# A fused attention and expert kernel: the convolution stage's operations in another order on three engines, and the row of maxima from a one-column stationary side

## The chip, the cores and the metric

The kernel runs on one core of one Trainium2 chip. A core has a matrix engine (TensorE, PE in the profile), three engines for elementwise work (VectorE or DVE, ScalarE or ACT, GpSimd or POOL), and a queue engine (SyncE or SP) that issues most of the DMAs. Each engine works through its own instructions strictly in the order in which they are written, and waits on semaphores for the others. The metric is the device time of one execution in microseconds (us), lower is better.

## The reference, cut to what matters

The input `x` has 8 images of 128 channels and 32x32 positions. A block with attention is added to it, then a block with routed experts. The change touches the attention block and where it meets the routing of the image before:

```python
inp = _ln_c(x) + 2.0 * sinu                     # per position, over channels
q = conv2d(inp, wq)                             # 1x1
k = conv2d(inp, wk, 1, 1); v = conv2d(inp, wv, 1, 1)   # 3x3, 128 -> 256 channels
q = q * cos + rotate_every_two(q) * sin         # the same for k
dots = einsum('bhid,bhjd->bhij', q, k) * SCALE  # 8 heads, 1024 x 1024 each
attn = softmax(dots, axis=-1)                   # subtracts each row's maximum
attn = einsum('bhij,hg->bgij', attn, mix)
out = einsum('bhij,bhjd->bhid', attn, v)        # then wo, bias and a sigmoid gate
x = x + a * sigmoid(g)                          # then tokens, router, two experts of 8
```

## The kernel before, in words

All matmuls are made precise by splitting every fp32 operand into a high part (`...h`, rounded to the engine's fast fp32 format) and a rest (`...l`), with three products instead of four. A copy on ScalarE makes the high part, a subtraction on VectorE the rest.

The eight images are eight batches of a loop (batch 0 stands alone in front of it, without the work on a batch before it). Each batch has two stages:

* **The convolution stage.** `conv_q` makes q in four pieces, `conv(b, cg, i)` the 3x3 convolutions in a Winograd form along x: `cg` is 0 and 1 for k's two halves of channels, 2 and 3 for v; `i` is one of four transformed components, each in its own bank of `ST`. A component is 9 matmuls for k and 18 for v. ScalarE copies component 0 out (`middle_copy`), VectorE joins the others (`middle_sums`, then `even_odd` for the even and the odd positions). For q and k, VectorE and GpSimd apply the rotary tables (`rotate` or `turn`, eight groups g: 0 to 3 are q, 4 to 7 are k), ScalarE and VectorE split the result (`rot_hi`, `rot_lo`) and SP spills it to DRAM (`stk`), from which `stacks` loads the operands of a head (`qst`, `kst`). Head 0 needs groups 0 to 5. For v, `v_hi` and `v_lo` split it in place. Woven into this stage is what is left of the batch before: `out_transpose`, `out_hi`/`out_lo`, `out_project`, `gate_tanh`/`gate`, `route_in`, `row_transposed`, `logits`, and the clearing of the accumulator `acc`.
* **The attention stage**, 32 units (8 heads by 4 blocks of 256 query rows), two heads to a call of `pair`. For each unit `max_scores` makes scores with the queries as the output's rows, `take_max` takes each row's maximum into `mcol`, `max_row` turns the column of maxima into a row by a matmul with a negative identity, ScalarE copies that row into `qst` (`row_copy`), `scores` makes the scores again, transposed and with the maximum subtracted, `exps` and `exp_lo` take exponentials and split them, `values` multiplies by v in 48 matmuls and `normalise` adds to the output through GpSimd.

The first two units' maxima and the first unit's scores and exponentials are made inside the convolution stage, between the components of v. `values` of unit 0 starts when all of v is split (`wait(pe, s_vlo, split)`). The order on each engine is written out by hand in the function `batch` of that engine; nothing reorders it later. Each engine's `batch` calls the helpers named above; the waits in them (`wait_ge`) count semaphore steps.

Of the kernel before, what the change touches and what calls it, by code (L numbers as in the profile page):

```python
# [43 lines left out]
def build(nc, x, wq, wk, wv, mix, wo, bo, wr, br, ln_g, ln_b, w1, b1, w2, b2,  # L44
# [19 lines left out]
    with ctx:  # L64
# [96 lines left out]
        mcol = a_sb("mcol", [P, 2, 2, P], f32r)  # L161
# [216 lines left out]
        def _(sp):  # L378
# [49 lines left out]
            def fill(i):  # L428
                if i == 0:
                    wait(sp, s_const, 11)  # L430
# [107 lines left out]
        def _(pool):  # L538
# [11 lines left out]
            nc.gpsimd.memset(f(mcol[:, :, :, :]), 0.0).then_inc(s_const, 1)  # L550
# [5 lines left out]
            pool.wait_ge(s_const, 11)  # L556
# [149 lines left out]
        def _(pe):  # L706
# [227 lines left out]
            def batch(b):  # L934
                prev = None if isinstance(b, int) else b - 1
                n = b * UNITS
                for g in range(4):
                    conv_q(b, g)
                if prev is not None:
                    out_transpose(prev, 0)  # L940
                conv(b, 0, 0)
                conv(b, 0, 1)
# [21 lines left out]
                max_row(n, 0)  # L964
                if prev is not None:
# [4 lines left out]
                conv(b, 3, 2)  # L970
                scores(n, 0, 0, b)
                conv(b, 3, 3)
                max_scores(n + 1, 1, 1)
                scores(n, 0, 1, b)
# [13 lines left out]
            pe.wait_ge(s_const, 8)  # L988
# [109 lines left out]
        def _(act):  # L1098
# [3 lines left out]
            act.wait_ge(s_const, 8)  # L1102
# [106 lines left out]
            def batch(b):  # L1209
                prev = None if isinstance(b, int) else b - 1  # L1210
                rot_hi(b, 0)
                if prev is not None:
                    out_hi(prev, 0)
                rot_hi(b, 1)
                rot_hi(b, 2)
                middle_copy(b, 0)
                rot_hi(b, 3)
                if prev is not None:
                    gate_tanh(prev, 0)
                    out_hi(prev, 1)  # L1220
                middle_copy(b, 1)
# [8 lines left out]
                rot_hi(b, 7)  # L1230
# [618 lines left out]
```

## Time and profile before

| | |
|---|---|
| time, median of 3 runs | 3048.92 us (3046.03 to 3050.79) |
| the profiled execution's own time | 3044.3 us |
| its span | 3042.6 us |
| TensorE busy | 2841.2 us (93%) |
| VectorE busy | 2269.0 us (75%) |
| ScalarE, GpSimd busy | 1469.0 us, 1395.8 us |
| mean granted TensorE clock | 0.969 of full speed |
| convolution stage of batch 1 | 358.2 to 421.5 us |
| the same stage of batch 2 | 683.7 to 747.0 us |

The span is the time from the first to the last instruction of the profiled execution. Batches 1 to 7 repeat each other every 326 us; after 2640 us follow the experts, which the change does not touch. A stage is taken here from the first matmul of `conv_q` to the first of `values`. Matmul rows overlap, so the time that a matmul takes of the engine is the distance between starts, not its duration. The granted clock is a share of full speed: 1.00 is 2.4 GHz, 0.50 is 1.2 GHz.

### The profile page before, as it was taken

The page shows a single profiled execution, that of the slowest core. Times are in us where ns is not written, and L with a number is a line of the kernel's source. Part 1 is how long each engine was busy: PE and PEld are TensorE (multiplying, and loading weights), DVE is VectorE, ACT ScalarE, POOL GpSimd, SP SyncE. Part 2 cuts the span into 40 slices and gives each one's busy share as a digit, 9 for nine tenths or more (in the row PEclk, how much of TensorE's full clock was granted, in tenths as well). Part 3 has the DMA queues.
Part 4 walks back from the last instruction along what each step waited for, and adds up shares of the span by engine and source line. Part 5 has one row for each costly group of instructions (what it writes and reads, how often), then busy time and mean ns, then how long its engine had stood idle before and what let it go on. Part 6 is the DMA issues. An engine that isn't in the chain of part 4 may idle for free.

```text
span 3042.6 us, 54782 instructions
## 1 busy us (share of the span) xinstructions
PE 2841.2 (93%) x20238; PEld 2665.9 (88%) x20238; DVE 2269.0 (75%) x3470; ACT 1469.0 (48%) x1884; POOL 1395.8 (46%) x1056
## 2 busy tenths in 40 slices
PE   6999989998999899999999899989998999958996
PEld 5899889997999899988998899979997999847776
DVE  6677778777877787777877787778777887655663
ACT  2455435543555355534554355535553455435771
POOL 4244524543454434552464245443455246336883
PEclk9999999999999999999999999999999999969998
DMA  2555020102010210102010211020011111137665
GB/s 110 189 195 200 29 73 22 37 18 91 22 38 26 77 36 24 41 31 72 22 45 11 89 32 30 25 91 22 25 39 56 47 32 59 43 115 250 231 223 210
DMA packets 88838, 230.51 MB, mean 76 GB/s; under 512 B 17160, under 2 KB 17746, under 8 KB 88566
## 3 DMA queue, kind: packets, MB, share of 16 engines
q1 hardware_dynamic: 79478, 209.96, 20.5%
q0 software_dynamic: 9088, 16.94, 1.7%
q8 instruction: 169, 2.77, 0.4%
q14 instruction: 103, 0.84, 0.1%
HBM read 90.76 MB, written 96.89 MB: 62 GB/s over the span
## 4 chain that ended last, share of the span: by engine, by line
PE 73%; issue 7%; DVE 7%; POOL 4%; DMA 4%; ACT 3%; SPq 1%; DVEq 0%; POOLq 0%; ACTq 0%
PE PV L708 46%; PE ST L708 14%; PE MX L708 12%; DMA wt<-wall 2%; DVE rt L1417 1%; POOL acc L587 1%; DVE ul L1370 1%; ACT h L1100 1%; DMA qst<-stk 1%; DMA stk<-rt 1%; ACT xr L1100 1%; DVE mcol L1448 1%; POOL rt L580 1%; POOL E L595 1%; POOL E L593 1%
## 5 line engine op out<-in xcount | busy, mean ns | idle before, releaser
L587 POOL TENSOR_TENSOR acc<-acc,tmp 128x256 f32<-128x256 f32 x512 | 802.8, 1568 | 1282.6 <-DVE tmp L1463 1280.3
L708 PE MATMUL PV<-vh,El 128*128 128x258 f32 x4096 | 1189.7, 290 | 27.5 <-DVE vl L1443 22.1
L708 PE MATMUL PV<-vh,Eh 128*128 128x258 f32 x4096 | 1162.1, 284 | 0.0
L708 PE MATMUL PV<-vl,Eh 128*128 128x256 f32 x4096 | 1152.2, 281 | 0.0
L1100 ACT ACTIVATE Eh<-ST 128x1024 fp32r<-128x1024 f32 x512 | 526.2, 1028 | 765.1 <-PE ST L708 765.1
L1448 DVE TENSOR_REDUCE mcol<-MX 128x1 fp32r<-128x1024 f32 x512 | 625.8, 1222 | 313.4 <-PE MX L708 310.6
L708 PEld LDWEIGHTS PV<-vh,El 128*128 128x128 f32 x4096 | 777.6, 190 | 59.4 <-DVE vl L1443 20.5
L708 PEld LDWEIGHTS PV<-vl,Eh 128*128 128x128 f32 x4096 | 783.4, 191 | 25.5 <-issue 3.8
L708 PEld LDWEIGHTS PV<-vh,Eh 128*128 128x128 f32 x4096 | 777.4, 190 | 0.0
L1453 DVE TENSOR_TENSOR El<-E,Eh 128x1024 fp32r<-128x1024 f32 x512 | 635.2, 1241 | 0.0
L1100 ACT ACTIVATE E<-ST 128x1024 f32<-128x1024 f32 x512 | 522.2, 1020 | 0.0
L708 PE MATMUL MX<-kst,qst 96*128 96x512 f32 x1024 | 331.2, 405 | 28.6 <-DMA qst<-stk 28.6
L708 PE MATMUL ST<-qst,kst 97*128 97x256 f32 x2048 | 343.2, 290 | 9.7 <-ACT qst L1100 6.7
L708 PEld LDWEIGHTS ST<-qst,kst 97*128 97x128 f32 x2048 | 281.7, 191 | 17.7 <-issue 9.5
L1463 DVE SCALAR_TENSOR_TENSOR tmp<-PV,rl,mix_sb 128x256 f32<-128x256 f32 x512 | 247.7, 484 | 18.8 <-DVE rl L1459 1.0
L674 POOL DMA_INDIRECT yrows<-xr,idx x156 | 189.6, 1216 | 76.5 <-issue 41.0
L1100 ACT ACTIVATE qst<-MX 1x256 fp32r<-1x256 f32 x256 | 96.8, 378 | 263.8 <-PE MX L708 263.3
L708 PEld LDWEIGHTS MX<-kst,qst 96*128 96x128 f32 x1024 | 160.7, 193 | 30.4 <-DMA qst<-stk 30.2
L1747 DVE TENSOR_TENSOR hl<-h,hh 128x1024 fp32r<-128x1024 f32 x78 | 95.7, 1227 | 102.6 <-ACT hh L1100 82.3
L1459 DVE RECIPROCAL rl<-PV 128x1 f32<-128x1 f32 x512 | 85.5, 167 | 102.3 <-PE PV L708 100.6
L593 POOL TENSOR_TENSOR E<-E,sin_sb 128x512 f32<-128x512 f32 x64 | 85.5, 1336 | 142.3 <-DVE E L1413 99.3
L611 POOL DMA_INDIRECT rows<-xr,slot x128 | 126.8, 991 | 27.0 <-issue 15.5
(245 smaller groups left out, 3476.8 us busy)
## 6 DMA issues: line engine op xcount, KB each, us to landing
rows<-xr SPq DMA_DIRECT2D x68, 520.0 KB, 6.2
stk<-rt SPq DMA_DIRECT2D x64, 512.0 KB, 2.7
kst<-stk SPq DMA_DIRECT2D x192, 128.0 KB
qst<-stk SPq DMA_DIRECT2D x192, 128.0 KB
wt<-wall SPq DMA_DIRECT2D x39, 514.0 KB
wt<-wall SPq DMA_DIRECT2D x39, 512.5 KB
xrow<-rows SPq DMA_DIRECT2D x39, 260.0 KB
wall<-yrows SPq DMA_DIRECT2D x32, 256.0 KB, 4.6
```

The source lines that it names most:

```text
L580: nc.gpsimd.tensor_tensor(u[3][:, :, 0:last], even[:, :, 0:last], even[:, :, 1:HALFW], ALU.subtract)
L587: nc.gpsimd.tensor_tensor(acc[:, ic, :], acc[:, ic, :], tmp[:, p, :], ALU.add).then_inc(s_acc, 1)
L593: nc.gpsimd.tensor_tensor(s, s, table(sin_sb, g), ALU.mult).then_inc(s_rot, 1)
L611: nc.gpsimd.indirect_dma_start(out=rows_d[:, :], out_offset=bass.IndirectOffsetOnAxis(ap=slot[:, i:i + 1], axis=0), in_=xr[c][:, g, :], in ...
L674: nc.gpsimd.indirect_dma_start(out=yrows_d[:, :], out_offset=bass.IndirectOffsetOnAxis(ap=idx[j % XR][:, i:i + 1], axis=0), in_=yrow[j % Y ...
L708: return nc.tensor.matmul(o, w, m, start=start, stop=stop)
L1100: return nc.scalar.activation(o, i, func, **kw)
L1448: nc.vector.tensor_reduce(mcol[:, k % 2, p, MROW:MROW + 1], MX[:, :], AX, ALU.max).then_inc(s_red, 1)
L1453: tt(El[at].rearrange("p a b -> p (a b)"), E32[:, p, :], f(Eh[at]).rearrange("p a b -> p (a b)"), ALU.subtract).then_inc(s_lo, 1)
L1459: nc.vector.reciprocal(rl[:, p:p + 1], PV[p][:, INNER:INNER + 1]).then_inc(s_rl, 1)
L1463: stt(tmp[:, p, :].rearrange("p (g d) -> p g d", d=DH), PV[p][:, 0:INNER].rearrange("p (g d) -> p g d", d=DH), rl[:, p:p + 1], m, ALU.mult ...
L1747: tt(low, exact, f(high), ALU.subtract).then_inc(t_hl, 1)
```

## The change

Three things are changed, and nothing in what is computed.

First, `mcol` holds only the maxima, two by two columns, where before it held a 128-column block for each with the maxima in column 96 and zeros elsewhere. `max_row` so loads one column as its stationary side and writes one row of `MX` (row 0) where it wrote 128 rows. The clearing of the block on GpSimd is gone, and the counts of `s_const` fall by one.

Second, `even_odd` is no longer called within `turn`; the clearing of `acc` is a function `clear`.

Third, the calls in the three `batch` functions stand in another order. Before and after (cut to the calls; those of the batch before have `prev`):

```diff
--- TensorE, batch(b)
-                for g in range(4):
-                    conv_q(b, g)
+                conv_q(b, 0)
+                conv_q(b, 1)
                     out_transpose(prev, 0)
+                conv_q(b, 2)
+                conv_q(b, 3)
                 conv(b, 0, 0)
+                    out_transpose(prev, 1)
                 conv(b, 0, 1)
                     out_project(prev, 0)
-                    out_transpose(prev, 1)
                 conv(b, 0, 2)
                 conv(b, 0, 3)
                 conv(b, 1, 0)
                 conv(b, 1, 1)
+                conv(b, 1, 2)
                     out_project(prev, 1)
-                conv(b, 1, 2)
                 conv(b, 1, 3)
                 conv(b, 2, 0)
                     route_in(prev)
                 conv(b, 2, 1)
+                conv(b, 2, 2)
+                conv(b, 2, 3)
                 max_scores(n, 0, 0, b * 384 + 96)
-                conv(b, 2, 2)
+                conv(b, 3, 0)
                 max_scores(n, 0, 1)
-                conv(b, 2, 3)
+                conv(b, 3, 1)
                 max_row(n, 0)
-                conv(b, 3, 0)
-                max_scores(n + 1, 1, 0)
-                conv(b, 3, 1)
                 conv(b, 3, 2)
                 scores(n, 0, 0, b)
+                max_scores(n + 1, 1, 0)
                 conv(b, 3, 3)
-                max_scores(n + 1, 1, 1)
                 scores(n, 0, 1, b)
+                max_scores(n + 1, 1, 1)
--- TensorE, max_row(n, k)
-                    last = mm(MX[:, p * P:(p + 1) * P], mcol[:, k % 2, p, :], negid[:, :], True, True)
+                    last = mm(MX[0:1, p * P:(p + 1) * P], mcol[:, k % 2, p:p + 1], negid[:, :], True, True)
--- ScalarE, row_copy(n, k)
-                copy(qst[st][MROW:MROW + 1, q * QT:(q + 1) * QT], MX[MROW:MROW + 1, 0:QT]).then_inc(s_mrow, 1)
+                copy(qst[st][MROW:MROW + 1, q * QT:(q + 1) * QT], MX[0:1, 0:QT]).then_inc(s_mrow, 1)
--- ScalarE, batch(b)
-                rot_hi(b, 0)
                     out_hi(prev, 0)
+                middle_copy(b, 0)
+                rot_hi(b, 0)
                 rot_hi(b, 1)
-                rot_hi(b, 2)
-                middle_copy(b, 0)
-                rot_hi(b, 3)
                     gate_tanh(prev, 0)
+                rot_hi(b, 2)
                     out_hi(prev, 1)
+                rot_hi(b, 3)
                 middle_copy(b, 1)
...
-                rot_hi(b, 7)
-                row_copy(b * UNITS, 0)
                 v_hi(b, 0)
                 v_hi(b, 1)
+                rot_hi(b, 7)
                 middle_copy(b, 3)
+                row_copy(b * UNITS, 0)
+                v_hi(b, 2)
+                act.wait_ge(s_rlo, b * 8 + 7)
                 exps(b * UNITS, 0, 0)
-                v_hi(b, 2)
                 v_hi(b, 3)
+                act.wait_ge(s_rlo, b * 8 + 8)
                 exps(b * UNITS, 0, 1)
--- VectorE, clear(n) and batch(b)
+            def clear(n):
+                wait(dve, s_tr, n * 4 + 4)
+                nc.vector.memset(acc[:, :, :], 0.0)
                 rotate(b, 0)
-                for g in range(1, 4):
-                    rotate(b, g)
-                    rot_lo(b, g - 1)
-                    if g == 1 and prev is not None:
-                        out_lo(prev, 0)
-                rot_lo(b, 3)
+                    out_lo(prev, 0)
+                rotate(b, 1)
+                    clear(prev)
+                rot_lo(b, 0)
+                rotate(b, 2)
+                rot_lo(b, 1)
+                rotate(b, 3)
                 middle_sums(b, 0)
+                even_odd(b, 0, 0)
+                rot_lo(b, 2)
                     gate(prev, 0)
+                turn(b, 4)
+                rot_lo(b, 3)
                     out_lo(prev, 1)
-                turn(b, 4)
+                even_odd(b, 0, 1)
                 turn(b, 5)
                 middle_sums(b, 1)
-                rot_lo(b, 4)
                     gate(prev, 1)
+                rot_lo(b, 4)
+                even_odd(b, 1, 0)
+                even_odd(b, 1, 1)
                 rot_lo(b, 5)
                 turn(b, 6)
                 turn(b, 7)
-                rot_lo(b, 6)
+                middle_sums(b, 2)
+                even_odd(b, 2, 0)
                     logits(prev)
+                rot_lo(b, 6)
+                v_lo(b, 0)
+                even_odd(b, 2, 1)
                 take_max(n, 0, 0)
-                middle_sums(b, 2)
+                v_lo(b, 1)
                 rot_lo(b, 7)
-                even_odd(b, 2, 0)
                 take_max(n, 0, 1)
-                even_odd(b, 2, 1)
-                    wait(dve, s_tr, prev * 4 + 4)
-                    nc.vector.memset(acc[:, :, :], 0.0)
-                v_lo(b, 0)
-                take_max(n + 1, 1, 0)
-                v_lo(b, 1)
                 middle_sums(b, 3)
                 even_odd(b, 3, 0)
+                take_max(n + 1, 1, 0)
+                v_lo(b, 2)
                 even_odd(b, 3, 1)
                 exp_lo(n, 0, 0)
-                v_lo(b, 2)
+                v_lo(b, 3)
                 take_max(n + 1, 1, 1)
-                v_lo(b, 3)
                 exp_lo(n, 0, 1)
```

How the instructions stand now is shown at three places of a batch of the loop. On VectorE at the head of the stage, from `rotate(b, 0)` on (`El<-PV` is `out_lo`, `rt<-E,rt` is `rot_lo`, `MEMSET acc` the clearing; ISA and REGISTER_ALU are the waits' own instructions), before:

```order
L1387 TENSOR_TENSOR E<-ST,cos_sb 128x512
L1388 STREAM_SHUFFLE E<-ST 128x512
L41 REGISTER_ALU
L1387 TENSOR_TENSOR E<-ST,cos_sb 128x512
L1388 STREAM_SHUFFLE E<-ST 128x512
L41 ISA
L1417 TENSOR_TENSOR rt<-E,rt 128x512
L41 ISA
L1424 TENSOR_TENSOR El<-PV,Eh 128x512
L41 REGISTER_ALU
L1424 TENSOR_TENSOR El<-PV,Eh 128x512
L41 REGISTER_ALU
```

After, from the shuffle of `rotate(b, 0)` on:

```order
L1393 STREAM_SHUFFLE E<-ST 128x512
L41 ISA
L1428 TENSOR_TENSOR El<-PV,Eh 128x512
L41 REGISTER_ALU
L1428 TENSOR_TENSOR El<-PV,Eh 128x512
L41 REGISTER_ALU
L1392 TENSOR_TENSOR E<-ST,cos_sb 128x512
L1393 STREAM_SHUFFLE E<-ST 128x512
L41 REGISTER_ALU
L1482 MEMSET acc 128x2048
L41 ISA
L1421 TENSOR_TENSOR rt<-E,rt 128x512
```

The two `out_lo` now stand before `rotate(b, 1)`, and the clearing, which stood behind both `even_odd(b, 2, ...)`, stands before the first `rot_lo`.

On VectorE at the end of the stage, from `middle_sums(b, 3)` on, before (`vl<-vt,vh` is `v_lo`, `mcol<-MX` is `take_max`, `El<-E,Eh` is `exp_lo`; `vt<-vt,ST` closes as `even_odd(b, 3, 1)`):

```order
L1394 TENSOR_TENSOR vt<-vt,ST 128x512
L1395 TENSOR_TENSOR vt<-vt,ST 128x512
L1399 REGISTER_ALU
L1402 TENSOR_TENSOR vt<-ST,vt 128x512
L1399 REGISTER_ALU
L1404 TENSOR_TENSOR vt<-vt,ST 128x512
L1453 TENSOR_TENSOR El<-E,Eh 128x1024
L1443 TENSOR_TENSOR vl<-vt,vh 128x512
L41 REGISTER_ALU
L1448 TENSOR_REDUCE mcol<-MX 128x1
L1443 TENSOR_TENSOR vl<-vt,vh 128x512
L1453 TENSOR_TENSOR El<-E,Eh 128x1024
```

After, from `even_odd(b, 3, 0)` on:

```order
L1407 TENSOR_TENSOR vt<-ST,vt 128x512
L41 ISA
L1452 TENSOR_REDUCE mcol<-MX 128x1
L1447 TENSOR_TENSOR vl<-vt,vh 128x512
L1404 REGISTER_ALU
L1409 TENSOR_TENSOR vt<-vt,ST 128x512
L1457 TENSOR_TENSOR El<-E,Eh 128x1024
L1447 TENSOR_TENSOR vl<-vt,vh 128x512
L41 REGISTER_ALU
L1452 TENSOR_REDUCE mcol<-MX 128x1
L1457 TENSOR_TENSOR El<-E,Eh 128x1024
```

Between `even_odd(b, 3, 1)` and the last `v_lo` stood an `exp_lo`, a `v_lo` and a `take_max`; now only the `exp_lo` stands there.

On TensorE at the end of the stage, from the last matmul of `conv(b, 3, 3)` to the first of `values`, before (`MX<-kst,qst` is `max_scores`, `ST<-qst,kst` is `scores`):

```order
L708 MATMUL ST<-wch,uh 128x256
L41 ISA
L708 MATMUL MX<-kst,qst 128x512 x2
L883 REGISTER_ALU
L708 MATMUL ST<-qst,kst 128x256 x4
L708 MATMUL PV<-vh,El 128x258
```

After:

```order
L707 MATMUL ST<-wch,uh 128x256
L882 REGISTER_ALU
L707 MATMUL ST<-qst,kst 128x256 x4
L41 ISA
L707 MATMUL MX<-kst,qst 128x512 x2
L707 MATMUL PV<-vh,El 128x258
```

`scores(n, 0, 1)` and `max_scores(n + 1, 1, 1)` have changed places.

## Rows read from the trace of the kernel before

**Rows 1.** Page, part 1: engine, busy us (share of the span), instructions.

```profile
PE 2841.2 (93%) x20238; PEld 2665.9 (88%) x20238; DVE 2269.0 (75%) x3470; ACT 1469.0 (48%) x1884; POOL 1395.8 (46%) x1056
```

**Rows 2.** Windows of batch 1: busy us of PE, PEld, DVE, ACT, POOL; PEclk, DMA, GB/s.

```profile
397.00:404.90 7.90, 5.58 (x22) 5.30 (x23) 4.65 (x7) 1.90 (x3) 2.45 (x2) 0.57 0.39 133
...
421.50:427.50 6.00, 6.00 (x35) 5.91 (x36) 2.44 (x3) 2.32 (x3) 0.00 (x0) 0.72 0.01 3
440.00:620.00 180.00, 179.04 (x1405) 174.53 (x1404) 146.31 (x228) 99.25 (x122) 90.28 (x62) 1.00 0.12 34
```

**Rows 3.** Waits of TensorE, whole run: total us, times, longest.

```profile
PE MX L708 <- DMA qst<-stk: 28.6, 8, 7.2
PE PV L708 <- DVE vl L1443: 22.1, 8, 2.9
```

**Rows 4.** Timeline of PE, batch 1: start, us, instruction, count [idle before <- releaser].

```profile
358.22 0.39 PE L708 MATMUL ST<-xl,wqh 128*128 128x512 f32 x1
...
399.32 1.22 PE L708 MATMUL MX<-kst,qst 96*128 96x512 f32 x2 [3.37 <-DMA qst<-stk]
400.33 0.41 PE L708 MATMUL ST<-wcl,uh 128*128 128x256 f32 x1
...
416.26 0.28 PE L708 MATMUL ST<-wch,uh 128*128 128x256 f32 x1
416.38 0.28 PE L708 MATMUL ST<-wcl,uh 128*128 128x256 f32 x1
...
418.03 0.74 PE L708 MATMUL ST<-qst,kst 97*128 97x256 f32 x4 [0.31 <-DVE vt L1404]
421.50 0.39 PE L708 MATMUL PV<-vh,El 128*128 128x258 f32 x1 [2.73 <-DVE vl L1443]
```

**Rows 5.** Timeline of DVE, same batch: the low half of group 5.

```profile
390.81 0.68 DVE L1417 TENSOR_TENSOR rt<-E,rt 128x512 fp32r<-128x512 f32 x1
```

**Rows 6.** Timeline of DVE: end of the stage.

```profile
417.29 0.69 DVE L1404 TENSOR_TENSOR vt<-vt,ST 128x512 f32<-128x512 f32 x1 [2.17 <-PE ST L708]
...
419.64 1.22 DVE L1448 TENSOR_REDUCE mcol<-MX 128x1 fp32r<-128x1024 f32 x1
420.77 0.68 DVE L1443 TENSOR_TENSOR vl<-vt,vh 128x512 fp32r<-128x512 f32 x1
```

**Rows 7.** Timeline of DVE: waits at the head, and the clearing.

```profile
360.62 0.68 DVE L1387 TENSOR_TENSOR E<-ST,cos_sb 128x512 f32<-128x512 f32 x1
...
365.47 1.03 DVE L1417 TENSOR_TENSOR rt<-E,rt 128x512 fp32r<-128x512 f32 x1 [2.27 <-ACT rt L1100]
...
372.82 1.01 DVE L1417 TENSOR_TENSOR rt<-E,rt 128x512 fp32r<-128x512 f32 x1 [1.83 <-ACT rt L1100]
...
408.34 1.76 DVE L1642 MEMSET acc<- 128x2048 f32 x1 [0.38 <-issue]
```

**Rows 8.** Timeline of DVE and POOL: two that meet.

```profile
387.22 1.82 DVE L1417 TENSOR_TENSOR rt<-E,rt 128x512 fp32r<-128x512 f32 x1
...
387.20 1.29 POOL L595 TENSOR_TENSOR E<-E 128x512 f32<-128x512 f32 x1
```

**Rows 9.** Timeline of PE round the row of maxima, full clock.

```profile
345.21 0.28 PE L708 MATMUL PV<-vh,Eh 128*128 128x258 f32 x1
345.34 0.33 PE L708 MATMUL MX<-negid,mcol 128*128 128x128 f32 x2
345.51 0.33 PE L708 MATMUL PV<-vh,El 128*128 128x258 f32 x1
345.68 0.28 PE L708 MATMUL PV<-vl,Eh 128*128 128x256 f32 x1
```

**Rows 10.** Windows of 75 us, one for each batch's stage.

```profile
358.20:433.20 75.00, 65.31 (x393) 57.90 (x392) 55.16 (x88) 22.49 (x34) 27.17 (x20) 0.93 0.27 92
...
1336.30:1411.30 75.00, 65.72 (x381) 58.02 (x381) 52.05 (x82) 22.10 (x33) 25.31 (x19) 0.91 0.27 92
```

**Rows 11.** Groups of weight loads: busy us, mean ns of one.

```profile
L708 PEld LDWEIGHTS MX<-negid,mcol 128*128 128x128 f32 x512 | 80.7, 192 | 0.0
```

More of the change, by code:

```diff
@@ L160, in build @@
         xg = a_sb("xg", [P, TOK], f32)
[L161 removed]
+        mcol = a_sb("mcol", [P, 2, 2], f32r)
         negid = a_sb("negid", [P, P], f32r)
@@ L429, in fill @@
                 if i == 0:
-                    wait(sp, s_const, 11)
+                    wait(sp, s_const, 10)
                 sp.dma_start(rows_d[i * FILL:(i + 1) * FILL, :].rearrange("(p r) c -> p (r c)", r=KC),
@@ L936, in batch @@
                 n = b * UNITS
-                for g in range(4):
-                    conv_q(b, g)
+                conv_q(b, 0)
+                conv_q(b, 1)
                 if prev is not None:
                     out_transpose(prev, 0)
+                conv_q(b, 2)
+                conv_q(b, 3)
                 conv(b, 0, 0)
+                if prev is not None:
+                    out_transpose(prev, 1)
                 conv(b, 0, 1)
@@ L960, in batch @@
                 max_scores(n, 0, 0, b * 384 + 96)
-                conv(b, 2, 2)
+                conv(b, 3, 0)
                 max_scores(n, 0, 1)
-                conv(b, 2, 3)
+                conv(b, 3, 1)
                 max_row(n, 0)
+                conv(b, 3, 2)
+                scores(n, 0, 0, b)
+                max_scores(n + 1, 1, 0)
+                conv(b, 3, 3)
+                scores(n, 0, 1, b)
+                max_scores(n + 1, 1, 1)
                 if prev is not None:
                     pe.wait_ge(s_lg, b + 0)
-                conv(b, 3, 0)
-                max_scores(n + 1, 1, 0)
-                conv(b, 3, 1)
-                conv(b, 3, 2)
-                scores(n, 0, 0, b)
-                conv(b, 3, 3)
-                max_scores(n + 1, 1, 1)
-                scores(n, 0, 1, b)
                 def heads_next(hp):
@@ L1210, in batch @@
                 prev = None if isinstance(b, int) else b - 1
-                rot_hi(b, 0)
                 if prev is not None:
                     out_hi(prev, 0)
+                middle_copy(b, 0)
+                rot_hi(b, 0)
                 rot_hi(b, 1)
-                rot_hi(b, 2)
-                middle_copy(b, 0)
-                rot_hi(b, 3)
                 if prev is not None:
                     gate_tanh(prev, 0)
+                rot_hi(b, 2)
+                if prev is not None:
                     out_hi(prev, 1)
+                rot_hi(b, 3)
                 middle_copy(b, 1)
@@ L1408, in turn @@
                 cg, odd = g // 2 - 2, g % 2
-                even_odd(b, cg, odd)
                 dve.wait_ge(s_rlo, b * 8 + g - 1)
@@ L1611, in batch @@
                 rotate(b, 0)
-                for g in range(1, 4):
-                    rotate(b, g)
-                    rot_lo(b, g - 1)
-                    if g == 1 and prev is not None:
-                        out_lo(prev, 0)
-                rot_lo(b, 3)
+                if prev is not None:
+                    out_lo(prev, 0)
+                rotate(b, 1)
+                if prev is not None:
+                    clear(prev)
[3 more added lines that the diff above has]
+                rotate(b, 3)
                 middle_sums(b, 0)
+                even_odd(b, 0, 0)
+                rot_lo(b, 2)
                 if prev is not None:
                     gate(prev, 0)
+                turn(b, 4)
+                rot_lo(b, 3)
+                if prev is not None:
                     out_lo(prev, 1)
-                turn(b, 4)
+                even_odd(b, 0, 1)
                 turn(b, 5)
                 middle_sums(b, 1)
-                rot_lo(b, 4)
                 if prev is not None:
                     gate(prev, 1)
+                rot_lo(b, 4)
+                even_odd(b, 1, 0)
+                even_odd(b, 1, 1)
                 rot_lo(b, 5)
```

10 lines of the change are left out of this document (4 added, 6 removed).

## The prediction

> **What bounds the kernel now.** First the page's part 1: TensorE is busy for 93% of the span, VectorE for 75% [rows 1]. Such shares are means over unlike stages, so next the windows by stage. In the attention loop TensorE is busy for 179.0 of 180 us at a granted clock of 1.00, VectorE for 146 [rows 2]: there only fewer or shorter matmuls count, and what VectorE or ScalarE do costs nothing. The convolution stage is different. The waits of TensorE over the whole run name two of its places, one each per batch: `max_scores` of unit 0 for the loads of head 0 (28.6 us in 8 waits) and the first `values` for the last low half of v (22.1 us in 8) [rows 3]. The timeline shows both in batch 1, 3.37 us ahead of 399.32 and 2.73 us ahead of 421.50 [rows 4]. Behind each the clock falls: 0.57 in the window that begins with the first wait, 0.72 behind the second [rows 2]. The stage goes from 358.22 to 421.50, 63.3 us [rows 4], eight times.
>
> **The head of the stage: reordered, worth nothing by itself.** It ends when `qst` and `kst` of head 0 have landed. That is 7.83 us (399.32 - 391.49) after VectorE ends the low half of group 5, at 390.81 + 0.68 [rows 4, 5]. So the question is when VectorE gets there. It starts at 360.62 and takes 30.9 us to that end, with waits of 2.27 and 1.83 us for ScalarE among them, and a third of the second's size [rows 7]; some 6 us in all. The new order puts more in front of that point: the clearing (1.7 us of the engine by its row of 1.76 [rows 7]) and both `even_odd(b, 1, ...)` (0.61 us each, the distance between starts of two such operations of 512 columns), 2.9 us. In return other work fills the old waits: `out_lo(prev, 0)` stands where `rotate(b, 0)` is being finished by GpSimd and ScalarE. One wait is new: `clear` needs all of `out_transpose(prev, 1)`, which on TensorE stands behind the transposes of the first half, two `conv_q` and `conv(b, 0, 0)` (0.85 + 1.4 + 2.05 us, from the starts of such matmuls in the timeline). I make that wait 1.7 us; behind it stand `rot_lo(b, 0)` and with it `rotate(b, 2)`, for which `conv(b, 0, 2)` waits, another 0.7 us on TensorE. With 2.9 added, about 2 of new waits and about 5 of old ones filled, VectorE ends group 5 when it did, to within 1.5 us. I take zero: the landing stays where it was.
>
> A rule of the Trainium skill, "SBUF — State Buffer", section "Who interferes with whom", speaks to this: the port pair that VectorE and GpSimd share is an exclusive lock, taken by a VectorE operation with two inputs in SBUF, and the later of the two stands still. The trace agrees: a `rot_lo` that takes 0.68 us elsewhere [rows 5] took 1.82 when GpSimd had started 1.29 us of work 0.02 us before it [rows 8]. The clearing now meets GpSimd's rotary work, and I take it to hold the lock like the others. By the rule a memset, which has no input, takes none; then the landing is about 1 us earlier than I take it, and the sum below would be 8 us less.
>
> **Between the landing and the first `values`: here is the gain.** Before, 22.2 us (399.32 to 421.50). A component of v is 18 matmuls at 0.12 us from start to start (416.26 to 416.38 [rows 4]), 2.14 us; four `max_scores` and two `scores` are 0.47 each, `max_row` 0.2. So 6 x 2.14 + 2.8 + 0.2 = 15.8 us of matmuls, waits of 0.31 + 2.73 = 3.0, some 2.7 lost to the low clock, 0.7 for latencies. After, `conv(b, 2, 2)` and `conv(b, 2, 3)` stand ahead of the landing, where TensorE waited: 4 x 2.14 + 3.0 = 11.6 us of matmuls remain. Their 4.3 us eat the old wait of 3.4 and what the head gives TensorE; I leave 1.1 us of wait there. Waits behind the landing, in the new order: `max_scores(n, 0, 1)` for `take_max(n, 0, 0)`, now behind `even_odd(b, 2, 1)`, 0.7; `scores(n, 0, 1)` directly behind `conv(b, 3, 3)` for `even_odd(b, 3, 1)`, 1.0; `values` for the last `v_lo`, 0.8. The last comes from VectorE's tail: from 417.29 to 421.45 before [rows 6], of which `v_lo` (0.61) and `take_max` (1.13, 419.64 to 420.77) no longer stand ahead of the last `v_lo`. Sum after: 11.6 + 2.5 + 0.7 = 14.8 us. Against 22.2 - 2.7 = 19.5 that is 4.7 us a batch without the clock. What was passed is late next: `take_max(n + 1, 1, 1)` comes after the start of `values`, and the `max_row` in it waits 0.4 us. Seven batches at 4.3 are 30 us. Batch 0, which had the longest wait of the eight (7.2 us [rows 3]), I put at 6. Together **36 us**.
>
> **The clock.** A window of 75 us over each stage has a mean granted clock of 0.93 (0.91 in one) [rows 10]: 75 x 0.07 = 5.2 us of full-clock time, 43 us over eight stages. Some of it falls into the waits themselves; what matmuls lose is about 34 us. It follows the two long waits. With 1.1 for 3.4 us at the first and three short ones for 2.7 at the second I expect most of it back, but not all, since the sparse matmuls of `route_in` and the short waits remain. Between 0 and 34 I take **20 us**.
>
> **The row of maxima.** 256 units. Before, from the start of its two matmuls to that of the second matmul behind them is 0.34 us, of which one matmul of 258 columns accounts for 0.12: the pair costs 0.22 [rows 9]. No row of this trace has a stationary side of one column. If loading it costs as before, nothing is gained. If it costs nothing, the pair is as long as its 256 moving columns, 0.12, and 0.10 us a unit or 26 us is gained. The matmul behind the pair still loads 128 columns, which 128 moving columns hardly cover; so I take the middle, 0.05 us, **13 us**.
> The Trainium skill, "TensorE: Matmul & The Clock Gate", section "LDWEIGHTS (loading the stationary operand)", has the load's time grow with its columns, 128 of them at 1.2 per ns, an estimate of 0.11 us. No row here shows one of another width. By it two of three loads vanish, and the saving would be 0.06 us a unit, 15 us.
>
> `row_copy` reads as many elements as before. The memset that goes on GpSimd lies in the setup, beside the loading of the weights: nothing.
>
> **Sum.** 36 + 20 + 13 = 69 us. The profiled execution took 3044.3 us, 4.6 below the median of 3048.92 and inside the spread of the runs. 3044.3 - 69 = **2975 us**.
>
> **The rivals.**
> A. The clock stays. The short waits that replace the long ones, with `route_in` between them, leave the clock as it was, and a narrow load costs what a wide one did. For it: the row at 0.91 against 0.93 [rows 10] shows that a stage can lose more with much the same waits. Against it: each low stretch of rows 2 begins at a wait of about 3 us. Time: 3044.3 - 36 = 3008.
> B. More than I take. The landing comes 1 us earlier, all of the clock returns, a unit saves 0.1: 44 + 34 + 26 = 104 us, 2940.
> C. The head becomes the bound. `clear` holds `rot_lo(b, 0)`, and what is behind it, for longer than the old waits give back, so that head 0 lands later by some 4 us. For it: that wait is new and in front of everything; against it: the 6 us that VectorE idled there. Each us later costs 8: 36 + 13 - 32 = 17, so 3027 with the clock unchanged. It would take 8 us a batch to undo all.
> D. Slower: the narrow load. A weight load is 192 ns long in its rows [rows 11] and runs beside the matmul ahead of it. If a load of one column, or the wide one behind it, can't be made ahead, each unit pays up to 2 x 0.19 us: 256 x 0.38 = 97 us. With 56 us of the other gains: 3044.3 - 56 + 97 = 3085. It decides from 0.22 us a unit on. For it speaks only that no row shows such a load.
> That the reordering does nothing at all would need the wait for `stk` to move with it; it doesn't hang on TensorE's order.
>
> **How the numbers follow.** My forecast 0.72, with its own range of 2955 to 2995 (head 1.5 us either way, 12 us; clock and row each by a third); A 0.13; B 0.07; C 0.05; D 0.03. The range from 2947 to 3012 takes in most of B and all of A. About 0.2% (6 us) is what a measurement of this kernel can tell from no change. Faster by more: 0.95; within it 0.02, from the edge between C and D; slower 0.03, D.
>
> **What would show it.** In the changed profile: the stage of batch 1 about 55 us long instead of 63.3; the wait of `MX` for `qst<-stk` about 1 us a batch, so 8 to 12 in all instead of 28.6, and that of `PV` for `vl` about 6 instead of 22; a wait of VectorE ahead of the clearing near 1.7 us; 14 to 16 us from the first `max_scores` to the first `values`; a granted clock of 0.96 or more in the 75 us; a unit of the attention loop shorter by about 0.05 us. I am wrong if the low half of group 5 ends more than 32.5 us after `rotate(b, 0)` starts, if the clock falls as often as before, or if a unit has become longer.

## The result, and the profile after

| | before | after |
|---|---|---|
| time, median of 4 runs each | 3047.48 us (3045.1 to 3050.79) | 2947.55 us (2941.37 to 2948.00) |
| profiled execution, its span | 3044.3, 3042.6 us | 2941.37, 2939.6 us |
| its mean granted clock | 0.969 | 0.983 |

The ratio is 0.9667, its interval 0.9652 to 0.9681: 100 us less, where my sum had 69 and the forecast was 2975 us. The time lies at the very edge of my range (2947) and outside the likeliest case's own (2955 to 2995). Counted from the 3044.3 us from which I had subtracted, the ratio gives 3044.3 x 0.9667 = 2943 us, and the profiled execution took 2941.37: both lie below the range. The direction and the places are as forecast, the size is that of rival B.

Part 1 of the page of after, beside [rows 1]:

```profile
PE 2785.8 (95%) x20238; PEld 2605.9 (89%) x20238; DVE 2268.5 (77%) x3470; ACT 1468.3 (50%) x1884; POOL 1405.3 (48%) x1055
```

TensorE's busy time is 55 us less with the same 20238 matmuls; the other half of the 103 us of span is idle time that is gone. 55 us less of busy time for the same work is already a hint at the clock and at the cheaper row. The profiled execution is the fastest of the four; the others had a mean clock of 0.981 and took 6 us more, so they may well hold a low stretch or two that this trace doesn't show.

Windows of batch 1 of after (busy us of PE, PEld, DVE, ACT, POOL; then clock, DMA share, GB/s). They answer to [rows 2], the last three to [rows 10]:

```profile
389.30:397.20 7.90, 7.84 (x63) 7.63 (x64) 5.61 (x8) 2.12 (x4) 0.00 (x0) 1.00 0.35 130
402.70:408.70 6.00, 5.83 (x46) 5.57 (x47) 4.79 (x6) 3.29 (x5) 0.53 (x1) 1.00 0.33 74
420.00:600.00 180.00, 178.95 (x1417) 173.81 (x1415) 147.64 (x229) 99.15 (x122) 91.03 (x63) 1.00 0.12 34
347.80:422.80 75.00, 70.15 (x465) 62.85 (x465) 64.04 (x108) 28.16 (x41) 29.60 (x22) 1.00 0.28 92
661.80:736.80 75.00, 70.59 (x464) 62.83 (x465) 62.68 (x105) 28.20 (x41) 30.27 (x22) 1.00 0.28 92
1289.40:1364.40 75.00, 70.55 (x463) 62.66 (x464) 62.75 (x105) 28.07 (x41) 30.48 (x22) 1.00 0.28 92
```

The two windows that stood at 0.57 and 0.72 stand at 1.00, and so do the 75 us of a stage that stood at 0.93 and 0.91. In the first, TensorE starts 63 matmuls in 7.9 us, where it started 22 before. The loop's 180 us are as full as they were; its matmuls are 1417 where they were 1405 in the same time, which is the cheaper row.

Waits of TensorE in after, beside [rows 3] (total us, times, longest):

```profile
PE MX L707 <- DMA qst<-stk: 10.5, 8, 3.2
PE ST L707 <- DVE E L1393: 10.2, 13, 1.4
...
PE ST L707 <- DVE vt L1409: 6.2, 8, 0.8
...
PE PV L707 <- DVE vl L1447: 4.8, 8, 0.7
...
PE MX L835 <- DVE xg L1441: 1.4, 1, 1.4
...
PE MX L707 <- DVE El L1428: 0.3, 1, 0.3
```

28.6 has become 10.5 and 22.1 has become 4.8; `scores(n, 0, 1)` now waits for `even_odd(b, 3, 1)`, eight times 0.8. The last two rows, together 1.7, are waits of the stage's head for work of the batch before; in the profile of before they were 7.7 and 15.2:

```profile
PE MX L708 <- DVE El L1424: 15.2, 14, 1.4
...
PE MX L836 <- DVE xg L1437: 7.7, 8, 1.4
```

I had not looked at these, since a longer wait stood behind them. They come back below.

TensorE's timeline, batch 1 of after: start, us, instruction, count [idle before <- releaser]. It answers to [rows 4]:

```profile
347.85 0.39 PE L707 MATMUL ST<-xl,wqh 128*128 128x512 f32 x1
...
351.24 1.09 PE L815 MATMUL PV<-ident,acc 128*128 128x128 f32 x8 [1.84 <-POOL acc L586]
...
372.00 0.49 PE L707 MATMUL MX<-El,woh 128*128 128x512 f32 x1 [0.35 <-DVE El L1428]
...
389.36 0.73 PE L707 MATMUL MX<-kst,qst 96*128 96x512 f32 x2 [1.09 <-DMA qst<-stk]
...
391.94 0.28 PE L707 MATMUL ST<-wch,uh 128*128 128x256 f32 x1
392.06 0.63 PE L707 MATMUL MX<-kst,qst 96*128 96x512 f32 x2
...
400.95 0.74 PE L707 MATMUL ST<-qst,kst 97*128 97x256 f32 x4 [0.78 <-DVE vt L1409]
401.53 0.63 PE L707 MATMUL MX<-kst,qst 96*128 96x512 f32 x2
402.74 0.36 PE L707 MATMUL PV<-vh,El 128*128 128x258 f32 x1 [0.58 <-DVE vl L1447]
```

The stage is 402.74 - 347.85 = 54.9 us long; 55 was forecast, for 63.3. The wait ahead of the first `max_scores` is 1.09, forecast 1.1. From there to `values` it is 13.38 us, forecast 14.8. `max_scores(n, 0, 1)`, at 392.06, follows the convolution with no wait at all.

VectorE in the same batch, beside [rows 5 to 8], and two rows of GpSimd:

```profile
350.25 0.68 DVE L1392 TENSOR_TENSOR E<-ST,cos_sb 128x512 f32<-128x512 f32 x1
...
357.13 1.76 DVE L1482 MEMSET acc<- 128x2048 f32 x1 [2.01 <-PE PV L815]
...
365.72 1.51 DVE L1436 TENSOR_SCALAR tmp<-tmp 128x512 f32<-128x512 f32 x1
...
380.68 0.69 DVE L1421 TENSOR_TENSOR rt<-E,rt 128x512 fp32r<-128x512 f32 x1
...
401.95 0.69 DVE L1447 TENSOR_TENSOR vl<-vt,vh 128x512 fp32r<-128x512 f32 x1
```

```profile
356.55 1.30 POOL L594 TENSOR_TENSOR E<-E 128x512 f32<-128x512 f32 x1
...
365.33 1.62 POOL L594 TENSOR_TENSOR E<-E 128x512 f32<-128x512 f32 x1
```

The clearing waits 2.01 us for the transposes (forecast 1.7), and the low half of group 5 ends 381.37 - 350.25 = 31.1 us after `rotate(b, 0)` starts, where it took 30.9: in this batch the head costs VectorE nothing, as forecast. The load lands 7.99 us later (7.83 before). Batch 1 is not like the others, though. In batches 2 to 7 the same way is 30.0 us long, where it was 30.9 in every batch of before, and the clearing waits less:

```profile
670.26 1.76 DVE L1482 MEMSET acc<- 128x2048 f32 x1 [1.29 <-PE PV L815]
```

To compare the variants I use three distances, from the starts in TensorE's timeline, as means over batches 1 to 7: from the stage's first matmul to the first `max_scores` ("to the landing"), from there to the first `values`, and from there to the third `max_row` (for e4 over six batches, since a record is missing in batch 4).

| us | to the landing | to `values` | stage | to third `max_row` | batch to batch |
|---|---|---|---|---|---|
| before | 42.05 | 21.52 | 63.57 | 18.91 | 326.20 |
| after | 41.30 | 13.39 | 54.68 | 17.13 | 313.88 |
| e1_row_only | 42.19 | 21.68 | 63.87 | 18.53 | 324.41 |
| e2_order_only | 41.34 | 13.45 | 54.78 | 17.49 | 316.24 |
| e3_filled | 44.99 | 19.73 | 64.71 | 16.94 | 325.54 |
| e4_early_max | 41.30 | 20.12 | 61.42 | 17.13 | 321.05 |
| e5_filled_ahead | 42.44 | 19.80 | 62.24 | 16.94 | 322.91 |
| e6_old_tail | 41.28 | 15.12 | 56.40 | 18.20 | 316.79 |
| e7_old_head | 43.56 | 14.20 | 57.76 | 17.29 | 317.33 |
| e8_clear_later | 41.83 | 13.38 | 55.21 | 17.31 | 314.88 |

### The profile page after: what moved, and what is told of

Same layout as the page of the kernel before. It is cut to its first block, busy times and chain, and to the rows that moved or that the text cites. A ratio compares the mean times of both kernels' runs of the same rounds, so it can differ in the third digit from the quotient of the medians.

```text
span 2939.6 us, 54790 instructions
## 1 busy us (share of the span) xinstructions
PE 2785.8 (95%) x20238; PEld 2605.9 (89%) x20238; DVE 2268.5 (77%) x3470; ACT 1468.3 (50%) x1884; POOL 1405.3 (48%) x1055
## 3 DMA queue, kind: packets, MB, share of 16 engines
q0 software_dynamic: 9088, 16.94, 1.8%
## 4 chain that ended last, share of the span: by engine, by line
PE 74%; DVE 8%; issue 5%; POOL 5%; DMA 4%; ACT 2%; SPq 1%; DVEq 0%; POOLq 0%; ACTq 0%
PE PV L707 48%; PE ST L707 14%; PE MX L707 11%; DMA wt<-wall 2%; DVE rt L1421 1%; POOL acc L586 1%; POOL E L594 1%; DVE ul L1375 1%; DMA qst<-stk 1%; DMA stk<-rt 1%; ACT xr L1102 1%; DVE El L1457 1%; POOL rt L579 1%; POOL E L592 1%; DMA wall<-yrows 0%
## 5 line engine op out<-in xcount | busy, mean ns | idle before, releaser
L707 PE MATMUL ST<-qst,kst 97*128 97x256 f32 x2048 | 337.0, 286 | 13.6 <-ACT qst L1102 7.4
L707 PE MATMUL MX<-kst,qst 96*128 96x512 f32 x1024 | 324.4, 398 | 10.5 <-DMA qst<-stk 10.5
```

Of the source, the lines that this page charges most:

```text
L707: return nc.tensor.matmul(o, w, m, start=start, stop=stop)
```

## The experiments

The median of before beside the first four was 3044.22 us, beside the other four 3044.38. My theory is that of the prediction, with larger sizes; the rivals are named in each expectation.

**The two parts, each alone.** `e1_row_only` is before with the one-column side alone; `e2_order_only` is after with the 128-column side put back:

```diff
--- e1_row_only, in before (mcol, row_copy and take_max to match)
-                    last = mm(MX[:, p * P:(p + 1) * P], mcol[:, k % 2, p, :], negid[:, :], True, True)
+                    last = mm(MX[0:1, p * P:(p + 1) * P], mcol[:, k % 2, p:p + 1], negid[:, :], True, True)
--- e2_order_only, in after: the same line the other way
```

> The kernel before with the one-column stationary side alone, order untouched. Theory (the narrow load is cheap): a unit of the attention loop, 7.90 us before and 7.83 in the changed kernel, becomes 7.83 here too; 256 units by 0.07 us is 18 us, so a ratio to before near 0.994, and the stage of batch 1 stays 63 us. Rival (the shorter unit comes from the order, the narrow side is worth nothing): ratio 1.000, unit 7.90.

> The changed order with the old 128-column stationary side. Theory: it gives what the whole change gives less 18 us: 2966 us, ratio 0.973; the stage of batch 1 54.9 us, no low clock in batches 1 to 7, a unit 7.90. If parts help each other (the short load keeps the clock up), low stretches come back here and the ratio is above 0.98.

Measured: e1 3027.81 us, ratio 0.9946 (0.9933 to 0.9959), 16 us less than before; e2 2965.48 us, 0.9743 (0.9728 to 0.9758), 79 us less. They add up: 16 + 79 = 95 of 100 us, within what the intervals (some 5 us each) can tell. So the row is worth 16 us in before and, between e2 and after, 18 (medians) to 23 (ratios). The place, in e1's timeline of TensorE, beside [rows 9]:

```profile
502.16 0.28 PE L707 MATMUL PV<-vh,Eh 128*128 128x258 f32 x1
502.28 0.28 PE L707 MATMUL MX<-negid,mcol 128*1 128x128 f32 x2
502.39 0.34 PE L707 MATMUL PV<-vh,El 128*128 128x258 f32 x1
502.56 0.28 PE L707 MATMUL PV<-vl,Eh 128*128 128x256 f32 x1
```

From the matmul ahead of the pair to the second behind it are 502.56 - 502.16 = 0.40 us, where [rows 9] have 0.47. That is 0.07 us a unit, 256 x 0.07 = 18 us. I had measured from the pair's own start and so left out 0.01 us ahead of it; the rest is that the middle of my bounds was a little low. The weight load, in the groups of after, beside [rows 11] (busy us, mean ns | idle):

```profile
L707 PEld LDWEIGHTS MX<-negid,mcol 128*1 128x1 f32 x512 | 41.4, 82 | 11.1 <-DVE mcol L1452 2.5
```

It lasts 82 ns where it lasted 192. By the Trainium skill, "TensorE: Matmul & The Clock Gate", section "LDWEIGHTS (loading the stationary operand)", 127 columns less at 1.2 per ns would be an estimated 106 ns less; the two rows differ by 110, so the trace agrees. Rival D is refuted: the pair has become shorter and not longer.

In one point e2 is not as expected: two of its seven windows of 75 us over a stage stand at 0.98 and not at 1.00. In batch 3 the low stretch is at the head of the stage, in batch 5 behind `values`, though the waits of these two stages (1.00 and 1.28, 0.78, 0.58 us) are about those of the other five.

**Is it the waits or the clock?** `e3_filled` and `e5_filled_ahead` are before with matmuls added whose result nobody reads, so that TensorE does not stand still at its two long waits:

```diff
+            def filler(count):
+                for i in range(count):
+                    mm(PV[1][:, :], wqh[:, 0:P], xh[:, 0:NB], True, True)
...
+                filler(12 if prev is not None else 28)      # e5: here
                 if prev is not None:
                     pe.wait_ge(s_xr, b + 0)
+                filler(13 if prev is not None else 29)      # e3: here instead
                 max_scores(n, 0, 0, b * 384 + 96)
...
                 scores(n, 0, 1, b)
+                filler(10)                                  # both
```

> The kernel before in its old order, with matmuls whose results nobody reads put into the two long waits of TensorE (13 of 512 columns ahead of the first max_scores, 29 in batch 0, and 10 ahead of the first values; 0.23 us each at full clock, so shorter than the waits of 3.4, 7.2 and 2.7 us). Nothing else is moved. Theory (the waits pull the clock down, and the low clock costs matmul time behind them): most of the 43 us by which the clock falls short over eight stages comes back, 25 to 34 us of it as time: 3015 to 3022 us, ratio 0.990 to 0.992, stage of batch 1 about 60.5 us. Rival (the clock falls for another reason, or what it costs is hidden by VectorE): ratio 0.999 to 1.001.

> The kernel before in its old order, with unread matmuls again, now ahead of TensorE's wait for ScalarE's copy of MX as well (in e3 they stood behind it, started 2.4 us late and ended after the loads of head 0 had landed): 12 of 512 columns ahead of that wait (28 in batch 0), 10 ahead of the first values. Theory (the waits pull the clock down and the low clock costs matmul time): the granted clock falls in fewer stages, the stage of batch 1 is 60.5 to 61 us, and of the 43 us lost in the clock 25 to 34 come back: 3012 to 3020 us, ratio 0.989 to 0.992. Rival (the low clock costs less, since TensorE waits for VectorE behind it anyway): the 15 us of e3 again, ratio 0.995.

Measured: e3 3028.8 us, 0.9949 (0.9933 to 0.9964), a miss by 7 us at least. The row that shows why, TensorE's timeline of e3:

```profile
395.79 2.50 PE L708 MATMUL PV<-xh,wqh 128*128 128x512 f32 x5 [2.38 <-ACT xr L1106]
```

My fillers stood behind TensorE's wait for ScalarE's `xr` copy, the `s_xr` of the diff. The profile of before puts the whole idle time down to the DMA, which came last; another semaphore was waited for in the same gap. So TensorE stood still for 2.38 us in spite of the fillers, and these then ran past the landing, which the table has at 44.99 instead of 42.05. So the total prices neither the waits nor the clock. The table does show the stretch behind the landing: 19.73 us to `values` instead of 21.52, and 16.94 instead of 18.91 from there.

e5 has them ahead of that wait: 3018.16 us, 0.9906 (0.9891 to 0.9921), as the theory had it (the stage of batch 1, 61.3 us, is a little longer than expected): 26 us less than before by the medians and 29 by the ratio, with more matmuls to do and the same work behind the same loads. Its timeline and its windows of 75 us over the stages of batches 1 and 3:

```profile
392.52 2.91 PE L708 MATMUL PV<-xh,wqh 128*128 128x512 f32 x12
396.44 0.74 PE L708 MATMUL MX<-kst,qst 96*128 96x512 f32 x2 [1.02 <-DMA qst<-stk]
```

```profile
354.90:429.90 75.00, 69.90 (x439) 60.97 (x439) 58.19 (x96) 24.45 (x36) 27.42 (x21) 1.00 0.27 92
...
999.70:1074.70 75.00, 69.82 (x425) 61.26 (x426) 55.54 (x88) 24.29 (x36) 26.55 (x20) 0.98 0.27 92
```

With the wait cut to 1.02 us the clock stays at 1.00 in five of the seven stages. That is shown, then: TensorE's standing still in the two long waits brings most of the low clock, and the low clock alone is worth 26 to 29 us here. This is a lower bound, for two reasons. Two stages (batches 3 and 6) still have a short stretch of it ahead of the landing, although no wait of over 1.8 us is in them. And the fillers push the first `max_scores` back by 0.4 us (42.44 for 42.05), some 3 us in the whole. The table gives the same size behind the landing: (21.52 - 19.80) + (18.91 - 16.94) = 3.7 us a batch, some 29 us in eight.

And since e5 and e2 both have the wide row and (nearly) no low clock, their distance is the worth of the order by itself: 3018.2 - 2965.5 = 53 us by the medians, 50 by the ratios; the 3 us of the fillers are in it, so it is rather 47 to 50.

**Two components of v ahead of the landing.** `e4_early_max` is after with the first `max_scores` back ahead of them:

```diff
-                conv(b, 2, 2)
-                conv(b, 2, 3)
                 if prev is not None:
                     pe.wait_ge(s_xr, b + 0)
                 max_scores(n, 0, 0, b * 384 + 96)
+                conv(b, 2, 2)
+                conv(b, 2, 3)
```

> The changed kernel with the first max_scores back ahead of conv(b, 2, 2), all else as changed. Theory (two components of v ahead of the landing are the main gain): TensorE waits 1.1 + 4.3 = 5.4 us there, low clock returns at that wait; 8 x 4.3 = 34 us and 15 to 20 for the clock: about 2998 us, ratio 0.983. Rival (the gain is in the tail and in the clock of the second wait): 2950 us, ratio 0.968.

Measured: 2998.41 us, 0.9853 (0.9834 to 0.9872), as expected: 51 to 57 us of the 100 hang on this one move. Timeline and window of its batch 1:

```profile
393.81 1.22 PE L707 MATMUL MX<-kst,qst 96*128 96x512 f32 x2 [5.51 <-DMA qst<-stk]
```

```profile
352.10:427.10 75.00, 65.72 (x410) 58.55 (x409) 56.58 (x93) 24.59 (x36) 26.63 (x20) 0.95 0.27 92
```

The landing has not moved (41.30 in both); what was work is a wait again, and behind the wait the clock falls.

**VectorE's tail.** `e6_old_tail` is after with the end of VectorE's stage as it was:

```diff
                 take_max(n + 1, 1, 0)
-                v_lo(b, 2)
                 even_odd(b, 3, 1)
                 exp_lo(n, 0, 0)
-                v_lo(b, 3)
+                v_lo(b, 2)
                 take_max(n + 1, 1, 1)
+                v_lo(b, 3)
                 exp_lo(n, 0, 1)
```

> The changed kernel with VectorE's old tail: v_lo(b, 2) and take_max(n + 1, 1, 1) back between even_odd(b, 3, 1) and v_lo(b, 3). Theory: the first values waits 2.3 instead of 0.58 us, 1.7 us in each of 8 batches is 14 us, and a low stretch returns behind that wait for 8 to 12 more: 2968 to 2974 us, ratio 0.975 to 0.977. If the tail's order is worth its own 1.7 us only, 2961 us, ratio 0.972. Rival (all of the gain is in the two components ahead of the landing): 2948 us, ratio 0.967.

Measured: 2971.91 us, 0.9755 (0.9742 to 0.9769), 24 us above after, or 27 by the ratios, as the theory had it.

```profile
408.25 0.56 PE L707 MATMUL PV<-vh,El 128*128 128x258 f32 x1 [2.31 <-DVE vl L1447]
```

```profile
407.70:413.70 6.00, 5.45 (x33) 5.30 (x34) 2.81 (x3) 2.15 (x3) 0.00 (x0) 0.72 0.13 29
```

The wait of `values` is 2.31 us instead of 0.58, which is 8 x 1.7 = 14 us, and the window behind it stands at 0.72, as the one of before did. The clock's part is again nearly as large as the wait's. It is not bound to each wait: in batch 5, with the same wait of 2.31 us, the clock stayed at 1.00.

**The head.** `e7_old_head` is after with the old head on all three engines, the clearing behind `rot_lo(b, 5)`; `e8_clear_later` is after with the clearing behind `rot_lo(b, 1)`:

```diff
--- e7_old_head, TensorE (ScalarE and VectorE likewise)
+                for g in range(4):
+                    conv_q(b, g)
                     out_transpose(prev, 0)
                 conv(b, 0, 0)
                 conv(b, 0, 1)
                     out_project(prev, 0)
+                    out_transpose(prev, 1)
...
+                    out_project(prev, 1)
                 conv(b, 1, 2)
--- e8_clear_later, VectorE
                 rotate(b, 1)
-                    clear(prev)
                 rot_lo(b, 0)
                 rotate(b, 2)
                 rot_lo(b, 1)
+                    clear(prev)
                 rotate(b, 3)
```

> The changed kernel with the old order of the head on TensorE, ScalarE and VectorE, up to the low half of group 5, turns with even_odd inside again, and the clearing right behind that low half. Theory of the prediction (the head's reordering moves nothing but the clearing): the loads land when they did, 41 to 42 us into the stage, but the clearing and both even_odd of k's second half now stand behind the landing's release and make groups 6 and 7 and take_max late, 2 to 2.5 us a batch: 2964 to 2970 us, ratio 0.974. Rival (the new head is what makes the rest early): the landing is 3 us or more later and the time above 2985 us, ratio above 0.98.

> The changed kernel with the clearing of acc behind rot_lo(b, 1) instead of ahead of rot_lo(b, 0), where VectorE waits 2.01 us for the transposes. Theory (GpSimd and ScalarE, not VectorE, set when groups 2 to 5 are done; the wait only moves to rot_lo(b, 0) and to conv(b, 0, 3)): same time within 3 us, 2945 to 2951. Rival (that wait is on the path to the landing): the landing comes up to 2 us earlier, TensorE's 1.1 us there go, 9 to 15 us less: 2933 to 2939 us, ratio 0.963.

Measured: e7 2972.53 us, 0.9754 (0.9739 to 0.9769), 25 us above after; e8 2952.31 us, 0.9691 (0.9677 to 0.9704), 5 us above it (7 by the ratios), at the edge of what can be told. So a later clearing does not bring the landing forward (41.83 against 41.30), and the wait ahead of the clearing costs nothing. e7 is the more telling one. It is a miss for both of its sides: 2.5 us above the theory's times, with the first `max_scores` at 43.56 and not at 41 to 42, and 12 us below the rival's. Waits with a bracket, and the first `max_scores`, in its batch 1:

```profile
352.52 1.10 PE L815 MATMUL PV<-ident,acc 128*128 128x128 f32 x8 [0.47 <-POOL acc L586]
358.62 0.50 PE L707 MATMUL MX<-El,woh 128*128 128x512 f32 x1 [0.90 <-DVE El L1424]
371.72 0.49 PE L707 MATMUL MX<-El,woh 128*128 128x512 f32 x1 [0.93 <-DVE El L1424]
381.83 1.09 PE L835 MATMUL MX<-ident,xg 128*128 128x128 f32 x8 [0.90 <-DVE xg L1437]
392.46 0.63 PE L707 MATMUL MX<-kst,qst 96*128 96x512 f32 x2
```

The first `max_scores` (392.46) has no wait for its loads any more: with the old head and two components more in front of it, TensorE itself gets there last. Now the small waits of the head count in full, 3.2 us in this batch, which in before were hidden in the wait for the landing. The new head has 1.84 + 0.35 = 2.2. Of the 2.9 us between the two arrivals (43.35 and 41.51 less the 1.09 of wait) these are 1.0; 7.4 x 0.22 = 1.6 are clock, which falls in this batch with hardly a wait:

```profile
379.00:385.00 6.00, 5.11 (x45) 4.90 (x44) 5.55 (x7) 0.63 (x1) 0.38 (x1) 0.98 0.46 175
385.00:392.40 7.40, 7.40 (x52) 7.40 (x52) 6.42 (x13) 2.62 (x4) 5.48 (x4) 0.78 0.38 106
```

Batches 2 to 6 are another case, and the more frequent one. Rows of batch 2, whose stage begins at 665.50:

```profile
675.84 0.50 PE L707 MATMUL MX<-El,woh 128*128 128x512 f32 x1 [1.40 <-DVE El L1424]
...
708.71 0.72 PE L707 MATMUL MX<-kst,qst 96*128 96x512 f32 x2 [0.40 <-ACT xr L1099]
712.39 0.72 PE L707 MATMUL MX<-kst,qst 96*128 96x512 f32 x2 [0.82 <-DVE mcol L1448]
```

The small waits of its head sum up to 3.9 us where batch 2 of after has 1.4, and that is 2.5 of the 2.7 us by which TensorE gets to the first `max_scores` later (42.8 us into the stage against 40.1). There it waits for ScalarE's `xr` copy and not for the loads, and the second `max_scores` waits for VectorE's `take_max`; both come late because of what now stands behind `rot_lo(b, 5)` on VectorE, as the theory had it for `take_max`: ahead of `xr` ScalarE copies out a component of v, and for that it waits 9.1 us for VectorE's `turn`, until 40.9 us into the stage (35.7 in after). With the wait for the landing (1.17) gone, that makes 1.9 us more to the first `max_scores` and 1.1 us more from there to `values`.

## Why the prediction was right in kind and wrong in size

By measured parts, in us (the parts were run on two occasions, so sums agree only to a few us):

| term | predicted | measured | from |
|---|---|---|---|
| order, without the clock | 36 | 50 to 53 (3 of them the fillers') | e5 against e2 |
| clock | 20 | 26 to 29 at least | before against e5 |
| row of maxima | 13 | 16 to 23 | e1; e2 against after |
| sum | 69 | 92 to 105 | the whole: 100 |

**The step that failed first: "Sum after: 11.6 + 2.5 + 0.7 = 14.8 us".** The matmuls were right. The waits behind the landing were to be 0.7 + 1.0 + 0.8; they are 0 + 0.78 + 0.58. And 13.38 - 11.6 - 1.36 leaves 0.4 for the latencies, not 0.7. Each price was rounded up a little, and the 1.4 us between 14.8 and 13.4 count eight times. The 19.5 that I had for the old stretch at full clock is 19.80 in e5, another 0.3. Together 1.65 us a batch, 13 us.

**The head: "I take zero: the landing stays where it was".** For batch 1, which I had read, it nearly holds: from the first `conv_q` 41.10 before, 41.51 after. For batches 2 to 7 it doesn't: they had it at 42.0 to 42.4 before, and have it at 41.0 to 41.6 after. The low half of group 5 in batch 2, VectorE's timeline of before and of after:

```profile
717.15 0.68 DVE L1417 TENSOR_TENSOR rt<-E,rt 128x512 fp32r<-128x512 f32 x1
```

```profile
694.51 0.68 DVE L1421 TENSOR_TENSOR rt<-E,rt 128x512 fp32r<-128x512 f32 x1
```

That is 33.42 us behind the stage's first matmul (683.73) before and 32.48 behind it (662.03) after, 0.9 us less. In batch 1 it was 32.59 and 32.83. VectorE was no quicker in batch 1 of before: from `rotate(b, 0)` to group 5 it took 30.9 us there as everywhere. But `rotate(b, 0)` starts 2.40 us into that stage and 3.2 to 3.5 us into the others, and in the new order these others get to group 5 in 30.0 us, with a shorter wait ahead of the clearing (1.29 for 2.01) and one slow `TENSOR_SCALAR` where batch 1 has two (below). So I had judged seven batches by the one that is unlike the rest. In e7, with the old head, group 5 ends 34.1 to 34.5 us into batches 2 to 7, in after 33.2 to 33.5. The head was worth 0.75 us a batch by itself, some 5 us. The heading "worth nothing by itself" is also wrong in a second way, which e7 shows: as soon as two components of v fill the wait, the head on TensorE is what the landing is waited out with, and the old one, with the clearing where e7 has it, costs 25 us. I had that in the sum ("what the head gives TensorE", 2.0 us; the wait left over, 1.1 forecast and 1.09 measured, was right), but hung none of the rivals on it.

**"The `max_row` in it waits 0.4 us": about right.** Between e5 and e2, both with the wide row, the way from `values` to the third `max_row` grows from 16.94 to 17.31 us in six of the seven batches; batch 5 of e2, with its low stretch, has 18.57 and makes the mean 17.49. Order per batch: 1.1 + 6.35 - 0.55 = 6.9 us where I had 4.3 (0.4 of the 1.1 are the fillers of e5); that is the 53 against 36, with 6.5 less 0.3 in batch 0's stage and attention.

**The clock: "Between 0 and 34 I take 20 us".** I expected most of it back but not all, because the sparse matmuls of `route_in` and the short waits remain. In the profiled execution batches 1 to 7 of after have no low window in their stages: with waits of 1.09, 0.78 and 0.58 us it all came back there. Only batch 0, with its wait of 3.2, still has a low stretch. My reason for the discount exists (e7's window at 0.78 behind `route_in`), if rarely: e2, with nearly the same waits as after, has a low stretch in two of seven batches, e8 in two. e4 and e6 show the other side: the waits put back bring low clock with them, in all seven batches of e4 and in six of seven of e6.

**The rule on the shared port.** In the trace the clearing (357.13, 1.76 us) meets GpSimd's 1.30 us that began at 356.55 and takes as long as it did alone [rows 7]. So the rule of the Trainium skill ("SBUF — State Buffer", section "Who interferes with whom") was right and my assumption that a memset holds the lock wrong. Whether the 8 us that I named for that case came from it is open: group 5 does come 0.9 us earlier in batches 2 to 7, but no run has the clearing hold the lock, so its part can't be told from that of the rest of the head. The gate lost some again: its `TENSOR_SCALAR`, 0.42 us in before, takes 1.51 beside GpSimd's work at 365.33 and 1.19 at the second place in batch 1; in batches 2 to 7 only the second one is slow (1.18):

```profile
L1432 DVE TENSOR_SCALAR tmp<-tmp 128x512 f32<-128x512 f32 x16 | 6.7, 418 | 6.1 <-ACT tmp L1100 6.1
```

```profile
L1436 DVE TENSOR_SCALAR tmp<-tmp 128x512 f32<-128x512 f32 x16 | 13.1, 822 | 5.6 <-ACT tmp L1102 5.6
```

These are the groups of before and of after; 16 times 0.4 us is the price of the new order there, less than 1 us a batch, and both stand ahead of the low half of group 5. The same section of the Trainium skill counts this kind of operation among those that can take the shared pair, so the trace agrees.

**The chances.** B was "the landing 1 us earlier, all of the clock, 0.1 a unit" at 0.07. Of its three conditions the clock came true (in the profiled execution), and the landing (0.75 us) and the unit (0.07) for the greater part; I had treated them as mishaps that must fall together, although each was an estimate of mine rounded to the careful side. Three careful roundings in one sum are no longer centred. A (the clock stays), C (the head becomes the bound) and D (the narrow load) are refuted: by the windows at 1.00, by the landing, and by e1.

## What to carry to other kernels

Where TensorE waits a few us once per pass, price the wait and the low clock that mostly follows it together: here a us put back into such a wait cost 1.5 to 1.9 us (e4: 4.4 us more wait a batch for 6.4 to 7.1 us of time; e6: 1.7 for 3.0 to 3.4). Fill such a wait with real work that is ready, and then look at the small waits ahead of it on the same engine, which the long one had been hiding. Read a repeated stage in several passes before taking its times as the loop's (here batch 1 was the odd one, before and in e7), and when every term of a sum was rounded the same way, move the forecast.

## What the hardware did that I had not expected

- The clock can fall while TensorE's row in the profile is full. In e7 the stretch from 385.0 to 392.4 us has TensorE busy for 7.40 of 7.40 us at a granted clock of 0.78. Ahead of it are a wait of only 0.90 us and 16 router matmuls, spread over 1.7 us (382.76 to 384.46). The same happens in batch 7 of e7 and not in its batches 2 to 6, and in after the same 16 matmuls, also 1.7 us, are followed by no low window. What decides between the two is left open.
- A clearing of 128x2048 on VectorE takes 1.76 us with and without GpSimd at work beside it, while a one-input `TENSOR_SCALAR` of 128x512 goes from 0.42 to 1.18 or 1.51 us.
- The clock does not fall behind every wait of the same length: in e6 `values` waits 2.31 us in seven batches and a low stretch follows in six.
- A weight load of one column lasts 82 ns, one of 128 columns 192 ns. In the stream of matmuls the pair with the narrow load saves 0.07 us: the matmul behind it still loads 128 columns.
